# A graph attention layer and a routed mixture of experts on one core: routing in three sets of tiles, residuals shared with GpSimd

## The reference

```
xn  = layernorm(x)
h   = xn @ W                       # 8 heads of 32
e   = leaky_relu(h.a_src[src] + h.a_dst[dst])
p   = exp(e - max(e));  s = segment_sum(p, dst)
gat = segment_sum(p / (s[dst] + 1e-10) * h[src], dst)
x1  = x + (gat + xn)
y0  = layernorm(x1)
logits = y0 @ gate_w + gate_b;  best two of 16 experts, softmax over the two
moe = sum over the two of weight * (relu(y0 @ w1[e] + b1[e]) @ w2[e] + b2[e])
out = x1 + layernorm(y0 + moe) * gamma + beta
```

## Time and profile before

| | |
|---|---|
| timed runs, us | 1995.39, 1995.41, 1996.13; median 1995.41 |
| profiled execution: first to last instruction | 1782.4 us |
| median less that span | 213.0 us |
| mean granted TensorE clock | 0.800 |
| busy in the span | PE 1417.7 (80%), DVE 1173.9 (66%), POOL 1206.3 (68%), ACT 775.1 (43%) |
| routing stage | 1153.8 to 1290.25 us of the span |

### The profile page before, as it was taken

The page is one execution under the profiler, slowest core; times in us unless marked ns, Lnnn a source line. Parts: engine busy times, 40 slices in busy tenths (PEclk is TensorE's granted clock), DMA queues, the critical chain, the costliest instruction groups (busy, mean ns, idle before and its releaser), DMA issues.

```text
span 1782.4 us, 28293 instructions
## 1 busy us (share of the span) xinstructions
PE 1417.7 (80%) x6757; PEld 1097.9 (62%) x6757; DVE 1173.9 (66%) x3565; ACT 775.1 (43%) x2345; POOL 1206.3 (68%) x1237
## 2 busy tenths in 40 slices
PE   4937877777777878778777877667699999999965
PEld 3725555545555555455554555466599999999953
DVE  6767777777777777777777777799734443332348
ACT  2634545455454545454454544444323333333335
POOL 3077777777777777777777777337457667656747
PEclk9957677777777776876777687855599999999987
DMA  6555555545554555554444445364579778878875
GB/s 199 182 143 132 138 134 137 134 133 137 134 137 133 139 132 138 133 134 137 132 139 132 139 131 142 100 213 148 143 213 223 212 207 218 212 201 212 212 182 184
DMA packets 166544, 284.22 MB, mean 159 GB/s; under 512 B 31743, under 2 KB 93268, under 8 KB 166228
## 3 DMA queue, kind: packets, MB, share of 16 engines
q0 software_dynamic: 62256, 143.99, 32.9%
q1 hardware_dynamic: 101764, 137.90, 25.7%
q10 hardware_dynamic: 2368, 0.52, 0.2%
HBM read 240.97 MB, written 42.16 MB: 159 GB/s over the span
## 4 chain that ended last, share of the span: by engine, by line
PE 41%; POOL 23%; DVE 14%; issue 11%; DMA 8%; DVEq 2%; ACT 0%; ACTq 0%; POOLq 0%; SPq 0%
POOL region L827 22%; PE bank L1104 11%; PE bank L1116 11%; PE bank L973 10%; DMA region<-node_rows,region 6%; DVE region L1421 3%; PE bank L962 2%; PE bank L906 2%; PE bank L1093 1%; DVEq L444 1%; DVE region L1367 1%; DVE region L1419 1%; DVE region L1804 1%; PE bank L1023 1%; DVE stats L1792 1%
## 5 line engine op out<-in xcount | busy, mean ns | idle before, releaser
L827 POOL DMA_INDIRECT region<-node_rows,region x832 | 788.9, 948 | 295.9 <-issue 227.9
L973 PE MATMUL bank<-region 128*128 128x264 f32 x1664 | 646.3, 543 | 0.2
L973 PEld LDWEIGHTS bank<-region 128*128 128x128 f32 x1664 | 421.9, 271 | 98.3 <-issue 6.3
L1421 DVE TENSOR_TENSOR region<-region,bank 128x264 f32 x728 | 309.7, 425 | 117.9 <-PE bank L973 61.1
L1407 DVE TENSOR_TENSOR region<-region,bank 128x512 f32<-128x512 f32 x416 | 282.1, 679 | 3.4 <-ACT bank L695 3.4
L678 ACT ACTIVATE region<-iota_row,region 128x128 f32<-128x128 f32 x832 | 262.5, 386 | 0.0
L754 ACT ACTIVATE region<-bank,b_col 128x128 f32<-128x128 f32 x452 | 128.8, 368 | 304.3 <-PE bank L1104 300.8
L887 POOL DMA_INDIRECT sum_rows<-region,row_u x113 | 179.4, 1587 | 104.9 <-DVE region L1775 40.6
L688 ACT ACTIVATE neg_max<-bank 128x1 f32<-128x1 f32 x104 | 17.8, 171 | 532.5 <-PE bank L998 532.5
L1104 PEld LDWEIGHTS bank<-region 128*128 128x128 f32 x1808 | 219.5, 192 | 6.3 <-DVE region L1732 0.5
L1104 PE MATMUL bank<-region 128*128 128x128 f32 x1808 | 220.2, 275 | 0.3 <-DVE region L1732 0.3
(11 more groups left out here) (242 smaller groups left out, 1539.9 us busy)
## 6 DMA issues: line engine op xcount, KB each, us to landing
region<-in_L_ffn_w SPq DMA_DIRECT2D x129, 512.0 KB, 5.0
region<-dloc_rows SPq DMA_DIRECT2D x104, 256.0 KB, 3.5
region<-node_rows,region POOLq DMA_INDIRECT x832, 2.8
node_rows<-region SPq DMA_DIRECT2D x12, 528.0 KB, 3.4
y_rows<-region SPq DMA_DIRECT2D x7, 896.0 KB, 6.0
sum_rows<-region SPq DMA_DIRECT2D x7, 896.0 KB, 7.6
region<-in_x SPq DMA_DIRECT2D x5, 896.0 KB, 8.6
region<-sum_rows SPq DMA_DIRECT2D x5, 896.0 KB, 11.0
```

Source lines behind the costliest of these rows:

```text
L827: p.indirect_dma_start(gathered[g % SLOTS][:, j, :], None, node_rows, bass.IndirectOffsetOnAxis(src_idx[:, k:k + 1], 0)).then_inc(row_in[g ...
L973: pe.matmul(bank[AGG_BANKS[k % AGG]][:, 0:ROW], onehot[:, (g % 3) * GROUP + j, :], gathered[g % SLOTS][:, j, :], start=True, stop=True).th ...
L1421: v.tensor_tensor(rows, rows, new, ALU.add).then_inc(acc_add)
```

## The change

The seven rounds of choice and places become three sets: batches 0 to 2, 3 and 4, 5 and 6. Each instruction of `choose` and `slots` spans a set's tiles (336 or 224 columns instead of 112); the one-hots stay by batch. Residuals and norms go by eight groups of 2, 5 and six times 7 tiles; VectorE forms groups 0, 1, 2 and 4, GpSimd 3, 5, 6 and 7. The inverse sums are taken in three parts (tiles 0 to 6, 14 to 48, 7 to 13). GpSimd makes the one-hots of batches 0 to 2 and VectorE those of 3 to 6. `pair_firsts` is one product and one sum for a set. `tile_1h` and the working tables of a set lie in the buffer that `b2` takes later, so `b2` is loaded in two parts behind them. The one-hots have three slots instead of two.

```
 A_TILES = (2, 5, 7, 7, 7, 7, 7, 7)
+C_TILES = (2, 5, 7, 7, 7, 7, 7, 7)
+C_DVE, C_POOL = (0, 1, 2, 4), (3, 5, 6, 7)
+C_PARTS = ((0, 7), (14, TILES), (7, 14))
+SETS = ((0, 3), (3, 5), (5, 7))
+POOL_HOTS = 3
...
 def sync_program(d):
-            d.dma_start(b2_bc, b2.rearrange("x f -> (x f)").partition_broadcast(P)).then_inc(b2_in, 16)
...
             for q in range(BATCHES):
-                d.wait_ge(residual_step, RESIDUALS * (q + 1))
+                store_y0(q)
+                i = q + 1
+                if i in C_POOL:
+                    d.wait_ge(x1_pool, 2 * C_POOL.index(i) + 2)
+                else:
+                    d.wait_ge(x1_dve, 2 * C_DVE.index(i) + 2)
                 while w2_at < behind_sums and ...:
                     load_w2(w2_at)
-                if q >= 1:
-                    store_y0(q - 1)
-            store_y0(BATCHES - 1)
             store_weights(0)
             store_weights(1)
+            d.wait_ge(tile_1h_ok, BATCHES)
+            d.wait_ge(pair_first_ok, len(SETS))
+            load_b2(0, b2_early)
+            d.wait_ge(table_mm, TILES)
+            load_b2(b2_early, EXPERTS)
...
 def scalar_program(s):
                 for t in range(t0, t0 + n):
                     s.activation(y_all[:, q % 2, t % BATCH, :], x_all[:, t, :], ACT.Identity, ...)
                     if t > t0:
                         copy_yt(t - 1)
+                    if i >= 2 and t == t0 + 3 and i + 1 < C_GROUPS:
+                        root_c(i + 1)
...
+            exp_gap(0)
+            copy_tables(0)
+            copy_tables(1)
+            exp_gap(1)
+            for q in range(2, BATCHES):
+                copy_tables(q)
...
 def gpsimd_program(p):
+            def residual(n):
+                i = C_POOL[n]
+                t0, t1 = c_first[i], c_first[i] + C_TILES[i]
+                hv = acc_t[:, t0:t1, 0:F_IN].rearrange("p t (h o) -> p t h o", o=F_OUT)
+                if n == 0:
+                    p.wait_ge(sums_step, SUMS["rsum", 1])
+                    p.wait_ge(s_ok, TILES)
+                p.tensor_tensor(hv, hv, rsum[:, t0:t1, :].unsqueeze(3).broadcast_to([P, t1 - t0, HEADS, F_OUT]),
+                                ALU.mult).then_inc(x1_pool)
+                p.wait_ge(x1_pool, 2 * n + 1)
+                p.tensor_tensor(x_all[:, t0:t1, :], acc_t[:, t0:t1, 0:F_IN], x_all[:, t0:t1, :],
+                                ALU.add).then_inc(x1_pool)
...
-            for q in range(BATCHES - 1):
+            for n in range(len(C_POOL)):
+                residual(n)
+            for q in range(POOL_HOTS):
                 choice_one_hots(q)
...
 def tensor_program(pe):
+            for i in range(C_GROUPS):
+                t0, t1 = c_first[i], c_first[i] + C_TILES[i]
+                for t in range(t0, t1):
+                    norm_transposes(t)
+                    if t > t0:
+                        gate_logits(t - 1)
+                    if i == 5 and t == t0 + 3:
+                        count_choices(0)
+                    if i == 7 and t == t0 + 3:
+                        count_choices(1)
+                gate_logits(t1 - 1)
+            choice_tables(0)
+            choice_tables(1)
+            count_choices(2)
+            for q in range(2, BATCHES):
+                choice_tables(q)
...
 def vector_program(v):
+            def best_two(s):      # the logits, max and index part of the former choose
+                t0, t1 = set_tiles(s)
...
+            def choose(s):        # its rest; slots(s) is the former slots without one-hots
...
+            def tile_hots(q):
+                v.wait_ge(choose_step, CHOOSE[s, "keyrow", 0])
+                if q >= 3:
+                    v.wait_ge(table_mm, (q - 2) * BATCH)
...
+            def slot_hots(q):
+                for k in range(TOP_K):
+                    v.tensor_tensor(slot_1h[:, sl, :, k, :], iota_b[:, :].unsqueeze(1).broadcast_to([P, BATCH, P]),
+                                    lo[:, k, t0:t0 + BATCH].unsqueeze(2).broadcast_to([P, BATCH, P]),
+                                    ALU.is_equal).then_inc(dve_1h_ok)
...
+            def pair_firsts(s):
+                n0, n1 = pairs_of(s)
+                junk_of_pairs = rank_all[:, 0:(n1 - n0) * 2 * EXPERTS].rearrange("p (n e) -> p n e", e=2 * EXPERTS)
+                v.tensor_tensor(junk_of_pairs, base[:, 2 * n0:2 * n1, :].rearrange("p (n t) e -> p n (t e)", t=2),
+                                pair_mask[:, :].unsqueeze(1).broadcast_to([P, n1 - n0, 2 * EXPERTS]),
+                                ALU.mult).then_inc(pair_mask_ok)
+                v.wait_ge(pair_mask_ok, s + 1)
+                v.tensor_reduce(pair_first[:, n0:n1], junk_of_pairs, AXIS_FREE, ALU.add).then_inc(pair_first_ok)
...
+            sums_part(0); inverse_sums(0); gathered_sums(0); add_x(0); stats_c(0)
+            sums_part(1); shift_c(0); inverse_sums(1)
+            gathered_sums(1); add_x(1); stats_c(1)
+            sums_part(2); inverse_sums(2); shift_c(1)
+            gathered_sums(2); add_x(2); stats_c(2)
+            stats_c(3, 2)         # with shift_c(2) behind its third tile
+            gathered_sums(4); shift_c(3); add_x(4)
+            stats_c(4); stats_c(5); shift_c(4); stats_c(6)
+            best_two(0); shift_c(5); choose(0)
+            stats_c(7); shift_c(6); slots(0)
+            tile_hots(0), tile_hots(1), tile_hots(2)
+            shift_c(7); pair_firsts(0)
+            best_two(1); choose(1); weights(0, 0); slots(1)
+            tile_hots(3); slot_hots(3); pair_firsts(1)
+            best_two(2); choose(2); weights(1, 0); weights(0, 1)
+            tile_hots(4); slot_hots(4); slots(2); weights(1, 1)
+            tile_hots(5); slot_hots(5); tile_hots(6); slot_hots(6)
```

More of the change, by code:

```diff
@@ L46 @@
 FC = HIDDEN // P
+assert sum(C_TILES) == TILES and sorted(C_DVE + C_POOL) == list(range(len(C_TILES)))
 assert TILES % BATCH == 0 and SLOT_TILES <= P and ROW <= 512
@@ L337, in pairs_done, with keep_of, logits_at, pairs_of @@
+        def keep_of(s):
+            return keeps[SETS[s][1] - SETS[s][0] - 2]
+        def logits_at(q):
+            s = set_of(q)
+            return 2 + s % 2, (q - SETS[s][0]) * BATCH * EXPERTS
+        C_GROUPS = len(C_TILES)
+        c_first = [sum(C_TILES[:i]) for i in range(C_GROUPS)]
+        def pairs_of(s):
+            done = [min(PAIRS, set_tiles(i)[1] // 2 + set_tiles(i)[1] % 2) for i in range(len(SETS))]
+            return (done[s - 1] if s else 0), done[s]
         def pairs_done(q):
@@ new lines, in norm_transposes, with count_choices @@
+            def norm_transposes(t):
+                pe.wait_ge(y0_ok, t + 1)
+                if t == 0:
+                    pe.wait_ge(gate_in, 32)
+                if t >= 2:
+                    pe.wait_ge(y0t_ok, t - 1)
+                for c in range(KC):
+                    ins = pe.transpose(bank[4 + t % 2][:, c * P:(c + 1) * P],
+                                       y_all[:, t // BATCH % 2, t % BATCH, c * P:(c + 1) * P], ident[:, :])
+                ins.then_inc(y0_tr)
+            def count_choices(s):
+                t0, t1 = set_tiles(s)
+                n = t1 - t0
+                pe.wait_ge(choose_step, CHOOSE[s, "masked" if s == LAST_SET else "both", 0])
+                if s >= 1:
+                    pe.wait_ge(choose_step, CHOOSE[s - 1, "rank", 0])
+                flat = both_all[:, 0:n * EXPERTS]
+                pe.matmul(bank[7][:, 0:n * EXPERTS], ones[:, :], flat, start=True, stop=(s == 0))
+                if s >= 1:
+                    pe.matmul(bank[7][:, 0:n * EXPERTS].rearrange("p (e t) -> p e t", t=n)[:, :, 0], ones[0:1, :],
+                              base[0:1, t0, :], start=False, stop=True)
+                pe.matmul(bank[6][:, 0:n * EXPERTS], before[:, :], flat, start=True, stop=True).then_inc(before_mm)
@@ new lines, in vector_program @@
+            add_x(4)
+            stats_c(4)
+            stats_c(5)
+            shift_c(4)
+            stats_c(6)
+            best_two(0)
+            shift_c(5)
+            choose(0)
+            stats_c(7)
+            shift_c(6)
+            v.wait_ge(pool_consts, POOL_CONSTS["empty"])
+            v.tensor_copy(empty, empty_i).then_inc(c_const_step)
+            slots(0)
+            for q in range(*SETS[0]):
+                tile_hots(q)
+            shift_c(7)
+            pair_firsts(0)
@@ L1655, in vector_program @@
+            best_two(1)
+            choose(1)
+            weights(0, 0)
+            slots(1)
+            tile_hots(3)
+            slot_hots(3)
+            pair_firsts(1)
+            best_two(2)
+            choose(2)
+            weights(1, 0)
+            weights(0, 1)
+            tile_hots(4)
+            slot_hots(4)
+            slots(2)
+            weights(1, 1)
+            for q in range(*SETS[2]):
+                tile_hots(q)
+                slot_hots(q)
             v.tensor_scalar(cnt_f[:, :], base[:, TILES, :], float(P - 1), None, ALU.add).then_inc(slot_step)
```

499 lines of the change are left out of this document (252 added, 247 removed).

## The result

The changed kernel takes 1989.28 us (median of six runs, 1986.72 to 1990.5), the kernel before on the same chip 1995.77: ratio 0.9965, 95% interval 0.9954 to 0.9975. The forecast was 1989.4. The number is right; two of its terms are not, and they cancel.

What follows compares the result with a forecast made beforehand. VectorE's program was taken to bound the routing stage: 118.3 us without waits, -22.4 work saved, +22.4 turns with GpSimd, +2.0 waits = 120.3 against 126.7; with +0.4 behind it -6.0, giving 1989.4 us, range 1972 to 2003.

Steps and rivals of the forecast that it cites:

- VectorE's own time: Routing stage: residuals -16.7, inverses -1.5, three sets -11.6, one-hots +7.6, norm group +0.6, pairs -0.8; sum -22.4 us.
- The turns: Residuals: GpSimd's eight 3.95 us instructions and VectorE's two-input instructions exclude each other; +22.4 us, last add at 47.5.
- my signs: Signs expected in the profile, among them VectorE's `var_eps` and `shift` far over 0.2 us.
- Rival D: GpSimd's residual instructions cost more than 3.95 us, feared for the zero-stride operand; at 5.7 us +14, 2003.4 us; chance 0.22.
- rival C: GpSimd's long instructions don't shut VectorE out, so the 22.4 us come back, less some 4: 1971 us; chance 0.18.
- The clock: Norm groups 3 to 7: TensorE, without gaps for 50 us, rises from 0.50 to 1.00, leaving 2.0 of 9.9 us of waits.
- rival B: The clock stays at 0.50 throughout the stage: 7.9 us more of VectorE's waits, 1997.3 us; chance 0.22.
- The walk: Stage from 1154.08 = 0: add starts at 47.5, VectorE works 22.6 us, then waits for counts until 74.4 (given as 3.3).
- b2: Its 2048 KB load, moved behind the last pairs, priced at nothing: hidden by slot products and TensorE's warm-up; without cover up to 6 us.
- the +0.4: Behind the stage's 1280.77 us mark: seven pairs in two dependent steps replace four, costing 0.4 us.
- My own sign for it: A growing gap from the last slot product to the first expert transpose would be `b2` and prove the forecast wrong.
- the 213 us: The 213.0 us by which the timed median (1995.4) exceeds the profiled span (1782.4) were taken to stay.

Runs made afterwards that it cites:

- e1: Kernel before, plus asserted bounds on the counts GpSimd loads before its scatters (edit shared by all these runs): 1791.2 us, ratio 1.0039 to the kernel before without it.
- e3: Changed kernel with the shared bounds edit and all eight residuals on VectorE, none on GpSimd: 1779.3 us, ratio 0.9966 to the kernel before; stage 114.4 us.
- e6: Against e3, one-hots of batches 3 to 5 go back to GpSimd (six batches there), all residuals on VectorE: ratio 1.0063 to the kernel before; stage 116.0 us.
- e2: Changed kernel with the shared bounds edit, otherwise unchanged: 1785.8 us, ratio 1.0004 to the kernel before; stage 119.0 us.
- e7: Against e4, each of the two b2 loads brings one expert only (256 KB in all): ratio 0.994 to the kernel before; counts to first transposes 13.8 us.
- e4: Against e2, GpSimd forms residual groups 5, 6, 7 only, each instruction started with VectorE's statistics or choice: 1775.3 us, ratio 0.9945 to the kernel before.

## Why the prediction was right, and where it was not

- **VectorE's own time.** Forecast for all but the residuals: -22.4 + 16.7 = -5.7 us. Measured between `e1` and `e3`, waits off (125.9 - 8.2 = 117.7; 114.4 - 3.6 = 110.8): -6.9. Sets, inverses, norm group and pairs together -13.9 (`e6`: 103.8 - 117.7) against -13.3 forecast (-1.5 - 11.6 + 0.6 - 0.8), one-hots +7.0 against +7.6. Right.
- **The turns.** Forecast +22.4 for -16.7 taken off; measured +17.6 for -16.2. The mechanism was right, as the earlier trace rows had it. The size was off since I priced product and sum at 3.95 each: the sum takes 3.98, the product 3.21, though it reads `rsum` through a stride of zero. Eight instructions need 4 x (3.21 + 3.98) = 28.8, not 31.6; from the first's start to the last's end there are 36.4 us, so VectorE's turns among them took 7.6, where I had 10.1. Hence the last add at 42.4 rather than 47.5. The rule of the Trainium skill, "SBUF — State Buffer", section "Who interferes with whom", is borne out by these rows (4.37 for 1.49, 5.69 for 2.01). It also names a `tensor_scalar` that uses both ports: `var_eps` was held too (1.63 for 0.17), as my signs had it. The sum has only 1.0 us for all small instructions. Rival D (5.7 us each) and its zero-stride fear are out by these prices, and rival C (no exclusion) by the rows above and by `e3`. That the turns, +22.4, had the very size of the sum of the parts, -22.4, was no rule at work: they are two separate sums.
- **The clock.** This step failed: "I take it that the clock rises here." It stayed at 0.50 through 40 us of 9.95 in 10 in the first profile, the condition of rival B, and in `e2` it rose for little more than 3 us. The waits were 8.7 us and 6.7, against the forecast's 2.0 and the 9.9 that B stood for. (The walk's own figures leave 4.3 us for the first of B's waits, 74.4 - 47.5 - 22.6, and not 3.3; it was 3.2 in both profiles.) My argument from the earlier trace rows compared stretches by how dense and how long they were, and not by what filled them: the one at 1.00 has products of 272 columns beside its transposes, the norms have products of 16 columns. Whether that is what decides was not tried alone. `e2` shows that the norm's work, though it fills TensorE, did not hold a clock that was at 1.00.
- **The errors cancel.** In the pair `e1`, `e2`: waits +4.7 over the forecast, turns -4.8, the residuals taken off +0.5, the rest of VectorE's own time -1.2, together -0.8, on a stage that had 0.6 less of VectorE's own time before (117.7 against 118.3). 120.3 - 0.8 - 0.6 = 118.9, and 119.0 were measured. That the first two are of one size is chance.
- **`b2`.** Priced at nothing, with "without cover up to 6": the stretch behind the counts grew by 1.1 us from `e1` to `e2` (0.9 between the first two profiles), and `e7` gives 1.3 back; so the +0.4 that I had there for the pairs is not to be seen. My own sign for it came true: from the end of the last slot product to the first transposes it took 6.0 us before and 6.6 after. The cover that I named, slot products and warm-up, is TensorE's; the first gather, on the DMA engines, had none.
- **What lies outside.** My reading of the 213 us was wrong, as told above; it moved no term, since the forecast was a difference.
- **What I did not ask** is whether the move of the residuals pays at all. My own sum had -16.7 against +22.4 for it, a loss of 5.7 us within a gain of 6.4. `e3` measures 4.7 in the stage. The rest of the change takes 11.5 us off the stage (125.9 in `e1`, 114.4 in `e3`).

## What to carry to other kernels

When two engines take turns, work moved from one to the other is gained only in stretches where the first does something that leaves the other alone: here statistics (3.0 us a group) and maxima. Start the moved instruction with that stretch; without those starts, the same six instructions made the stage 11 us longer. An instruction longer than the stretch is paid for at its end (the five `var_eps` of `e4`); cutting it to the stretch's length was not tried. In a forecast, sum each part of a change by itself, and if a part comes out negative, say so: a good total can hide it.

## What the runs showed of the hardware

- GpSimd's f32 `tensor_tensor` over 1792 columns: 3.21 us for the product with a zero-stride operand, 3.98 for the sum of two plain inputs; the first was priced the dearer one in rival D.
- VectorE's `var_eps`, a `tensor_scalar` of 5 or 7 columns with one input, is held up as well (1.63 and 1.41 us for 0.17 in the first profile). Inside GpSimd's instructions a reciprocal of 56 columns (0.50), `bn_stats` (0.39), `bn_aggr` (0.16) and, in `e4`, `max` (1.70 for 21) kept their usual times.
- Busy time of a VectorE that stands behind GpSimd counts as work: 109.8 us in `e2` with 17.6 of standing, 108.0 in `e3` without GpSimd's residuals and with 16.2 us more to do.
- TensorE can be busy 9.95 of 10 us and be granted 0.50: here with f32 transposes of 128x128 and products of 16 columns, in all profiles of the changed kernel. In `e2` a clock at 1.00 fell to 0.50 during such work, without a gap.
- The asserted bounds of some register loads on GpSimd cost 5.8 us in the expert stage (424.0 against 418.2); the whole program took 1.0039 times as long.
